# Batch 1 of a two-layer attention and expert kernel in two halves of its token tiles from the last self-attention on, in a new order of steps

## What is computed

```python
x = x + L0_xattn(layernorm(x), ctx, ctx)          # 16 heads of 8, 77 keys, projection Wo
x = x + L0_ffn(layernorm(x))                      # router, top 2 of 8 experts, relu squared
x = x + L1_xattn(ctx, layernorm(x))               # 16 heads, 77 keys, then a layernorm
x = x + L1_ffn(layernorm(x))                      # self-attention over 512 tokens, then experts
...
def L1_ffn(src):
    q, k, v = heads of src@Wq, src@Wk_c@Wk, src@Wv_c@Wv ; rope on q and k
    x = rmsnorm(src + softmax(q k^T / sqrt(8)) v @ Wo, norm1_w)
    shared = swiglu(x @ W_shared_in) @ W_shared_out
    w = gates of 2 groups x 4 experts, top 2       # softmax, argmax, one-hot
    h = swiglu(x @ W1_shared)
    out = x + shared + sum_e (h @ W2_experts[e]) * w[e]
    return rmsnorm(out, norm2_w)
```

## Time and profile before

| what | us |
|---|---|
| median of 3 runs (343.17 to 344.15) | 343.85 |
| the profiled execution's own time | 343.82 |
| its span, first to last instruction | 342.0 |
| PE / DVE / ACT / POOL busy in the span | 310.9 / 269.2 / 213.4 / 70.8 |
| mean granted clock of PE, as a share of 2.4 GHz | 0.975 |

### The profile page before, as it was taken

How to read it: one execution, slowest core, us unless ns; L and a number is a source line. 1 busy time by engine, 2 the same in 40 slices (tenths; PEclk the granted TensorE clock), 3 DMA queues, 4 the chain that set the end, 5 groups by cost and what they waited for, 6 DMA issues and landing times.

```text
span 342.0 us, 6013 instructions
## 1 busy us (share of the span) xinstructions
PE 310.9 (91%) x2257; PEld 157.3 (46%) x2257; DVE 269.2 (79%) x687; ACT 213.4 (62%) x260; POOL 70.8 (21%) x130
## 2 busy tenths in 40 slices
...
DMA packets 1900, 7.48 MB, mean 22 GB/s; under 512 B 208, under 2 KB 336, under 8 KB 1488
## 3 DMA queue, kind: packets, MB, share of 16 engines
...
...
## 4 chain that ended last, share of the span: by engine, by line
PE 55%; DVE 22%; issue 10%; ACT 9%; POOL 1%; DMA 1%; POOLq 0%; SPq 0%; ACTq 0%; DVEq 0%
PE ring_ps L597 32%; PE out_ps L597 11%; DVE mx L1189 8%; ACT pT L973 5%; PE misc_ps L597 4%; DVE ACC L1365 3%; PE misc_ps L813 2%; PE ring_ps L720 1%; PE misc_ps L758 1%; DVE ACC L1038 1%; PE misc_ps L633 1%; DVE Z L1038 1%; DVE bn L1048 1%; DMA rows<-in_rows 1%; ACT qT L965 1%
## 5 line engine op out<-in xcount | busy, mean ns | idle before, releaser
L973 ACT ACTIVATE pT<-ring_ps 128x1024 f32<-128x1024 f32 (+1 forms) x96 | 94.3, 1027 | 24.2 <-PE ring_ps L597 23.3
L1189 DVE TENSOR_REDUCE mx<-ring_ps 128x2 f32<-128x1024 f32 (+1 forms) x96 | 98.8, 1075 | 7.7 <-PE ring_ps L597 7.2
L597 PE MATMUL ring_ps<-XT,f 128*128 128x512 f32 x96 | 44.3, 601 | 0.0
L526 POOL TENSOR_TENSOR rstd<-var,consts 128x4 f32<-128x4 f32 x14 | 14.8, 1056 | 134.8 <-DVE var L1056 73.9
L597 PE MATMUL out_ps<-pT,V 128*32 128x512 f32 x256 | 34.9, 605 | 0.0
L565 POOL TENSOR_SCALAR pT<-pT 77x1024 f32<-77x1024 f32 x8 | 22.7, 2848 | 47.4 <-ACT pT L973 47.4
L597 PE MATMUL ring_ps<-f,hid 128*128 128x512 f32 (+1 forms) x96 | 31.9, 486 | 0.0
L1365 DVE SCALAR_TENSOR_TENSOR X<-ring_ps,gw,X 128x128 f32<-128x128 f32 x64 | 18.0, 345 | 16.8 <-PE ring_ps L597 16.5
L597 PEld LDWEIGHTS ring_ps<-f0y,hid 128*128 128x128 f32 x256 | 29.6, 192 | 2.4 <-issue 1.9
L597 PE MATMUL ring_ps<-f0y,hid 128*128 128x128 f32 x256 | 30.4, 276 | 0.0
L597 PE MATMUL ring_ps<-kT,qT 48*128 48x512 bf16 x128 | 24.1, 384 | 2.3 <-DVE mx L1189 1.3
...
## 6 DMA issues: line engine op xcount, KB each, us to landing
f<-in_f SPq DMA_DIRECT2D x1, 1669.0 KB, 14.1
...
rows<-in_rows SPq DMA_DIRECT2D x1, 512.0 KB, 10.3
trig<-in_trig SPq DMA_DIRECT2D x1, 512.0 KB, 10.6
...
```

What stands on the lines that cost most here:

```text
L526: return pool.tensor_tensor(out, a, c, op)
L597: return nc.tensor.matmul(out, lhsT, rhs, start=start, stop=stop)
L973: nc.scalar.activation(probs_buf(layer, i, kt)[0:parts_, 2 * half:2 * half + 2, :], ring_ps[ring.buf(step)][0:parts_, :, :], ACT.Exp, scal ...
L1189: V_.tensor_reduce(dst, src, AX.X, ALU.max).then_inc(ring.read_sem(step), 1)
```

## The change

The constant `HALVED = {1}` names the batches that are taken in halves. `PARTS` is then 0, 1 and 3: batch 0 whole, batch 1's tiles 0 and 1 (part 1) and its tiles 2 and 3 (part 3). `group_of` gives the tiles of a group of heads: i = 4 to 7 is now the first half of batch 1, and new groups i = 12 to 15 are the second.

For batch 1, from the scores of layer 2 to the store:

- SMAX is done per tile as before, so a half-group has 4 of its 8 steps, and then its own MCH, MTR (4 transposes, not 8), OC and OTR (2, not 4). There are 12 of each in layer 2 instead of 8.
- ST covers all four heads and 256 tokens in one step: four matmuls of 256 columns fill the same ring buffer that two of 512 filled, and one exponential of 1024 elements a row writes four pieces of `pT`. The number of ST steps stays 64. A PV step has 256 columns; there are 48 instead of 32.
- XT z2, OP, STAT/NORM r1, XT fl, GT, GTE, GH, SO, STAT/NORM r2 and OUT are done once for each half, on two tiles (GH and SO with half the columns). RO was already made of two tiles. The store is three DMAs, not two.

The order of steps is a new one over the whole kernel, with new lists of dummy matmuls (60 + 37 = 97) and of steps that borrow the ring. In it, among others: layer 0's batch 0 goes through OP, the norm and all its experts (FH, FY 0) while layer 0's batch 1 has four groups still to finish; layer 1 of batch 0 and the experts of batch 1 follow; layer 2 of batch 0 is prepared before layer 1 of batch 1; GH 0 0 stands after most of the second half's maxima, and batch 0's experts and the first half's stages stand among the second half's ST and PV.

```diff
+HALVED = {1}
...
+    GTE 0, OC 2 12, ST 2 13 1 0, ST 2 13 2 0, GH 0 1, GH 1 0, PV 2 13 1, SMAX 2 15 3 0, ST 2 13 3 0, PV 2 13 2,
+    GT 1, GTE 1, ST 2 14 0 0, OC 2 13, ST 2 14 1 0, PV 2 13 3, RO 0 0 0, PV 2 14 0, PV 2 14 1, MCH 2 15,
+    SMAX 2 15 3 1, RO 0 0 1, ST 2 14 2 0, RO 0 1 0, MTR 2 15, ST 2 14 3 0, RO 0 1 1, STAT r2 0, PV 2 14 2,
+    ST 2 15 0 0, OTR 2 12, OC 2 14, ST 2 15 1 0, PV 2 14 3, PV 2 15 0, ST 2 15 2 0, ST 2 15 3 0, PV 2 15 1, SO 1,
+    PV 2 15 2, NORM r2 0, OTR 2 13, PV 2 15 3, OUT 0, OC 2 15, OTR 2 14, OTR 2 15, GH 1 1, XT z2 3, OP 2 3,
+    STAT r1 3, NORM r1 3, RO 1 0 0, XT fl 3, GH 3 0, GT 3, GTE 3, GH 3 1, RO 1 0 1, SO 3, STAT r2 1, RO 3 1 0,
+    RO 3 1 1, STAT r2 3, NORM r2 1, OUT 1, NORM r2 3, OUT 3
...
+def part_of(h):
+    b = h % B
+    return b, tuple(range(2 * (h // B), 2 * (h // B) + 2)) if b in HALVED else tuple(range(T))
+
+def group_of(layer, i):
+    b, g = divmod(i % NGRP, GR)
+    return b, g, part_of(b + B * (i // NGRP))[1] if layer == 2 else tuple(range(T))
+
+PARTS = tuple(h for h in range(2 * B) if h < B or h % B in HALVED)
...
             def ST(step, layer, i, kt, half):
...
+                if len(tiles) < T:
+                    for r in range(2):
+                        for k in range(2):
+                            rows_ = slice(HS * k, HS * k + SROWS)
+                            last = mm(ps[:, k, 2 * P * r:2 * P * (r + 1)], kT[b][rows_, 2 * g + r, kt * P:(kt + 1) * P],
+                                      qT[b][rows_, 2 * g + r, tokens(tiles)])
+                    last.then_inc(ring.full_sem(step), 1)
+                    return
...
             def PV(step, layer, i, kt):
...
-                    last = mm(out_ps[j * VW:(j + 1) * VW, :], vals, probs_buf(layer, i, kt)[0:keys, j, :],
+                    last = mm(out_ps[j * VW:(j + 1) * VW, 0:len(tiles) * P], vals,
+                              probs_buf(layer, i, kt)[0:keys, j, 0:len(tiles) * P],
                               start=(kt == 0), stop=(kt == NKT[layer] - 1))
...
             def GH(step, b, w):
...
                     for c in range(2):
-                        last = mm(ps[:, c, :], win[:, w, 2 * half + c, :], XT[b][:, :])
+                        last = mm(ps[:, c, 0:len(tiles) * P], win[:, w, 2 * half + c, :], XT[b][:, tokens(tiles)])
```

More of the change, by code:

```diff
@@ L84 @@
 SCALE = (DH ** -0.5, 1.0, DH ** -0.5)
 ORDER = """
[L107 to L130, removed]
```

336 lines of the change are left out of this document (204 added, 132 removed), and 3 rows, old and new, of the table KEPT_BUSY.

## The result

The changed kernel takes 351.67 us (median of 4 runs, 350.73 to 353.52) against 344.0 us before (343.17 to 344.7): ratio 1.021, 95% interval 1.017 to 1.026. The forecast was 340.8 and the range ended at 351, so direction and range were wrong. The profiled execution has a span of 348.9 us against 342.0; its granted clock is 0.991 on average, before it was 0.975, so the clock is not the cause. In all comparisons here the median is that of all runs, and the ratio leaves out the few that ran over 1.5% longer than the fastest of their kernel.

What follows compares the result with a forecast made beforehand. The prediction saw limits differing by stretch, with ACT leading before GH 0 0 and PE full after. Its stretches, 162.5 + 104 + 39 + 33.5, gave a 339.0 us span and a forecast of 340.8 us, range 331 to 351.

Steps and rivals of the forecast that it cites:

- what bounds the kernel: Opening step, whole kernel: limits differ by stretch; PE stands 22.8 us before GH 0 0, ACT leads from 227.3 to 282.9.
- (1): Layer 2's batch 1, same work in two halves: ST +1.3 us, PV +1.3, small steps +0.4 on PE.
- (2): Gates of layer 2's batch 1: one more GT and GTE, +4.9 us on DVE.
- (3): ACT's silus and exponentials alternate: 7 table loads after the first instead of 2, +6.4 us, hidden; uncovered 1.28 each.
- (5): New order up to SMAX 2 0 0 0: that step comes at 162.5 us, not 167.1.
- R3: Rival, slower: clock drops in the new hand-over and the old one cost 4 to 6 us; 346 us, chance 0.07.
- (6): SMAX 2 0 0 0 to GH 0 0: ACT relieved, DVE last; 104 us instead of 115.8.
- (7): GH 0 0 to the last PV: PE-bound, 39 us, with PE busy 38.4.
- (8): Tail after the last PV: 33.5 us, against 54.5 before.
- R1: Rival, slower: behind GH 0 0 PE stands for DVE's gate chains and last SMAX steps; 348 us, chance 0.21.
- R2: Rival, slower: attention keeps its pace, SMAX 2 0 0 0 to GH 0 0 stays 115.8 us; 352 us, chance 0.08.

Runs made afterwards that it cites:

- e10: Kernel before, with each PV of layer 2's batch 1 computed for 256 of its 512 columns: 343.36 us, ratio 0.994.
- e11: Kernel before, with each exponential of layer 2's batch 1 taken of half the columns: 343.23 us, ratio 0.996.
- e15: Kernel before, with the score maxima of layer 2's batch 1 taken of half the keys: 344.78 us, ratio 0.999.
- e13: Order of the kernel before up to SMAX 2 4 0 0, its later steps kept later, then batch 1 in halves: 352.92 us, ratio 1.021.
- e3: Changed kernel, with an exponential in place of silu in the GH halves, so ACT never changes table there: 350.01 us, ratio 1.015.

## Why the prediction was wrong, point by point

The sum was 339.0 us of span and the span is 348.9. Its terms: SMAX 2 0 0 0 at 163.5 (forecast 162.5), from there to GH 0 0 109.6 (104), to the last PV's end 43.1 (39), and 32.7 behind it (33.5).

**The step that failed is the first one, what bounds the kernel.** The prediction counted PE's work from 167.1 to GH 0 0 with 0.22 us for each ST and SMAX step, came to 93.0 us, and concluded that PE stands 22.8 us there and that ACT bounds the second part. The earlier trace rows said otherwise beside it: PE busy 55.08 + 54.33 = 109.4 of 115.8. When a sum of prices and the busy time of the same stretch differ by 16 us, the prices are wrong. From start to start ST and SMAX take 0.31 to 0.32 in the trace of before when a PV or a transpose follows them and 0.23 otherwise; the 0.20 of the earlier trace rows is that of two equal steps in a row. Counted from start to start in the trace, the 128 ST and SMAX steps of layer 2 from 167.1 to GH 0 0 hold 38.7 us of PE's busy time, where 0.22 gives 28.2; that is 10.6 of the 16. The dummies hold 14.2 instead of 10.3, and the rest is in other steps. With PE busy 54.3 of 55.6 us from 227.3 on and all of the 48.7 behind it, little was there to be relieved: e10, e11 and e15 show that even a large cut on one engine gave 2.0, 1.1 and 0.4 us.

**(1) Same work in two halves.** Forecast +1.3 for ST, +1.3 for PV, +0.4 for the small steps, 3.0 in all; e13 shows 5.4. ST was no dearer than whole (12.1 us for all ST steps from SMAX 2 4 0 0 on, in both). PV cost 1.4 more (24.2 against 22.8; a halved one is 0.57 and not 0.54). The small steps made the difference: MTR 0.33 and OTR 0.37 for a half against 0.55 and 0.54 whole, that is +0.4 and +0.8 for four groups; XT, OP, GH, SO and GT together +1.5. RO, which is no smaller than before, costs +0.8 for all eight: batch 0's four take 3.54 to 3.63 from start to start, where attention steps stand between them, and 3.44 before, where there are none. That these steps are the reason is read from the rows and was not tried. One more dummy and SMAX share 0.7. The bounds had taken this in; what turned it into time is that it was added to a full engine.
**(2) GTE.** Right: 4.0 us for the half (291.92 to 295.95), and it stayed off the path.
**(3) Table loads.** Seven, as forecast. "Hidden, uncovered 1.28 each" was half right: 2.1 us of 9. Of the 2.66 us that the Trainium skill, ScalarE: Activation LUTs, "What ACT_TABLE_LOAD costs", gives for a load and a drain, only the load showed: at 277.20 it took 1.28, and the next instruction began at 278.50.
**(5) The order up to SMAX 2 0 0 0.** Right in size (-3.6 against -4.6), and R3 did not come (granted clock 1.00 from 50.7 to 340.9). But the milestone was the wrong one: it had been reached by leaving DVE and PE work behind it, and at SMAX 2 4 0 0 0.7 us were left of it.
**(6) To GH 0 0.** 5.6 us over the forecast. 1.9 of them are POOL's guards, which the prediction had costed at nothing because POOL is at 21%. The rule stands in the Trainium skill, SBUF — State Buffer, "SBUF: two separate sides": DVE and GpSimd share one port pair as a lock; whichever starts first, a GpSimd instruction or a DVE one in a two-port mode or with two SBUF inputs (the latter only against a GpSimd instruction that reads SBUF), keeps the other out to its end. The trace agrees in part. The two `rinv` instructions end with a guard (0.83 us instead of 0.17, ending at 173.88, the guard at 173.86; 0.52 us, ending at 184.18, the guard at 184.15), and the maxima, which read PSUM, stayed at 1.21 beside the same guards. But Z, with two SBUF inputs, was lengthened to 0.81 us and ended at 175.01, while the guard beside it ran until 176.6; by the rule it would have ended after the guard (spans on POOL are rough in the profile). Behind SMAX 2 4 0 0 the stretch was bound by PE (41.77 of 42.60) and not, as forecast, by DVE (39.15). How the other 3.7 us divide between that and DVE's waits for PE ahead of it was not settled.
**(7) GH 0 0 to the last PV.** PE-bound, as forecast, but PE was busy 41.56 and not 38.4; 1.4 of the 4.1 us are table loads (e3). It also holds 13 PV steps and not the 12 that were counted, 0.57 us; the rest goes with the prices of (1).
**(8) The tail.** Right: 32.7 against 33.5.
**The rivals.** R1 had the right sign, with 348, for a reason that the trace doesn't bear out: DVE was not what PE stood for behind GH 0 0 (0.2 us of waits), PE was simply longer. The first part of R2, that the attention keeps a pace which halving doesn't change, was nearer than the forecast: 6 us gained of 12. That its 352 meets the measured 351.67 is luck: it came to it with (6) at 115.8, which took 109.6, and with (7) as forecast, which took 4.1 more.
